# A recommendation tower on one core: what GpSimd does between rows of five gathers

## The reference, cut to what matters

```python
e = jnp.stack([tbl_0[ids[:, 0]], tbl_1[ids[:, 1]], ..., tbl_31[ids[:, 31]]], axis=1)   # 2048 x 32 x 16
row, col = _pair_indices(32)                                # the 496 pairs i < j
z = jnp.sum(e[:, row, :] * e[:, col, :], axis=2)
h = jnp.concatenate([z, dense_ctx], axis=1)                 # 2048 x 512
h = jnp.maximum(h @ W_top1 + b_top1, 0.0)                   # 512
h = jnp.maximum(h @ W_top2 + b_top2, 0.0)                   # 256
y = h @ W_top3                                              # 2048 x 1
```

## Time and profile before

| What | us |
|---|---|
| median of 3 runs | 390.6 |
| lowest, highest | 388.05, 390.77 |
| the profiled execution, whole time | 392.31 |
| its span, first to last instruction | 390.5 |
| TensorE matmuls busy, x2748 | 301.6 |
| VectorE busy | 248.0 |
| GpSimd busy | 227.9 |
| ScalarE busy | 145.0 |
| mean granted TensorE clock | 0.921 |

### The profile page before, as it was taken

The page is one execution under the profiler, slowest core; times in us unless marked ns, Lnnn a source line. Parts: engine busy times, 40 slices in busy tenths (PEclk is TensorE's granted clock), DMA queues, the critical chain, the costliest instruction groups (busy, mean ns, idle before and its releaser), DMA issues.

```text
span 390.5 us, 7439 instructions
## 1 busy us (share of the span) xinstructions
PE 301.6 (77%) x2748; PEld 278.9 (71%) x2748; DVE 248.0 (63%) x326; ACT 145.0 (37%) x311; POOL 227.9 (58%) x250
## 2 busy tenths in 40 slices
PE   1658697999777967977796797879679786978377
PEld 1348696888776857977785797768579776877366
DVE  6798769565956567394647739464673946556541
ACT  3982443434442424344242434424243441113012
POOL 6446655566656656665665666566566656657700
PEclk9988899899998999889899988989998898999759
DMA  6770020202020200102030110202012000000000
GB/s 140 207 236 5 8 64 6 65 6 64 8 63 5 64 6 15 53 6 63 5 64 6 24 44 6 63 6 64 6 17 51 6 6 5 7 8 6 7 3 1
DMA packets 19036, 14.51 MB, mean 37 GB/s; under 512 B 9727, under 2 KB 16461, under 8 KB 19022
## 3 DMA queue, kind: packets, MB, share of 16 engines
q1 hardware_dynamic: 10284, 11.69, 9.9%
q0 software_dynamic: 7680, 1.98, 6.5%
q10 hardware_dynamic: 1058, 0.66, 0.6%
HBM read 14.24 MB, written 0.08 MB: 37 GB/s over the span
## 4 chain that ended last, share of the span: by engine, by line
POOL 24%; PE 24%; issue 20%; DMA 11%; DVE 7%; another core or an unknown queue 6%; ACT 6%; SPq 1%; POOLq 0%; DVEq 0%; ACTq 0%
POOL emb L367 24%; DMA emb<-tbl,idx 10%; PE bank L663 7%; PE bank L683 6%; PE bank L645 5%; DVE emb L470 2%; PE bank L642 2%; ACT distance L844 2%; PE bank L780 1%; DVE prod L480 1%; DVE prod L489 1%; PE bank L692 1%; PE bank L699 1%; DVE mask L438 1%
## 5 line engine op out<-in xcount | busy, mean ns | idle before, releaser
L367 POOL DMA_INDIRECT emb<-tbl,idx x240 | 226.7, 945 | 141.8 <-DMA emb<-tbl,idx 80.1
L489 DVE TENSOR_TENSOR prod<-emb,bank 128x1904 f32<-128x1904 f32 (+5 forms) x51 | 94.5, 1854 | 99.3 <-DMA emb<-tbl,idx 97.3
L663 PE MATMUL bank<-ident,prod 128*128 128x128 f32 x768 | 101.9, 286 | 11.6 <-issue 4.5
L663 PEld LDWEIGHTS bank<-ident,prod 128*128 128x128 f32 x768 | 94.1, 197 | 14.3 <-issue 5.7
L683 PE MATMUL bank<-zT,w_sb 128*128 128x128 f32 x480 | 73.4, 303 | 17.7 <-ACT zT L882 16.5
L645 PE MATMUL bank<-parts,onehot 125*128 125x160 bf16 (+1 forms) x816 | 84.8, 239 | 1.8 <-issue 1.7
L683 PEld LDWEIGHTS bank<-zT,w_sb 128*128 128x128 f32 x480 | 65.9, 213 | 21.5 <-issue 19.8
L645 PEld LDWEIGHTS bank<-parts,onehot 125*128 125x128 bf16 x816 | 68.0, 104 | 1.2 <-issue 0.7
L642 PE MATMUL bank<-far_ten,named_ten 100*128 100x160 bf16 x160 | 40.9, 256 | 36.1 <-issue 26.6
L470 DVE TENSOR_REDUCE emb<-bank 128x480 f32 (+5 forms) x96 | 52.6, 583 | 10.3 <-remote 4.3
L875 ACT COPY bank<-emb 128x112 f32 (+3 forms) x32 | 7.8, 243 | 107.7 <-issue 68.4
(11 more groups left out here) (71 smaller groups left out, 137.4 us busy)
## 6 DMA issues: line engine op xcount, KB each, us to landing
gids<-small_ids_f SPq DMA_DIRECT2D x16, 544.0 KB
emb<-tbl,idx POOLq DMA_INDIRECT x240
w_sb<-w SPq DMA_DIRECT2D x1, 1024.0 KB
w_sb<-w SPq DMA_DIRECT2D x1, 512.0 KB
tab<-tbl SPq DMA_DIRECT2D x7, 56.0 KB
tab<-tbl SPq DMA_DIRECT2D x5, 70.0 KB
tab<-tbl ACTq DMA_DIRECT2D x5, 70.0 KB
z_last<-dense SPq DMA_DIRECT2D x16, 8.0 KB
```

What stands on the lines that cost most here:

```text
L367: nc.gpsimd.indirect_dma_start(emb[:, t, at:at + D], None, tables[f], bass.IndirectOffsetOnAxis(ap=idx[:, t, f:f + 1], axis=0)).then_inc(d ...
L489: return nc.vector.tensor_tensor(prod[:, at * D:(at + n * a) * D].rearrange("p (j i d) -> p j i d", j=n, d=D), strided(emb_at(t, PLACES[g] ...
L663: mm = nc.tensor.matmul(bank[:, Z_BANK + place, c * P:(c + 1) * P], v[:, d, :], ident[:], start=(d == 0), stop=(d == D - 1), is_transpose= ...
```

## The change

The wait for the landing of each fifth gather is taken out. In its place GpSimd makes six writes (memsets) of 128 x 16 float32 zeros into a new buffer `pace` that nobody reads, alternating between its two halves. Each write raises the semaphore `paced` when it is finished, and GpSimd waits for that before its next instruction. The condition on the tile changes too: the pause now stands after places 4, 9 and 14 of every tile except after place 14 of the last tile, so the last tile gets two pauses that it did not have. The number of pauses is 45 in tiles 0 to 14 as before, and 2 more; the number of writes is 47 x 6 = 282.

```diff
 RUN = 5
+WRITES = 6
...
+        pace = sb("pace", [P, 2, SUB])
...
+        paced = sem("paced")
...
                         place = GROUP_AT[g] + i - S
-                        if t < LAST_TILE and place % RUN == RUN - 1:
-                            pool.wait_ge(done, 16 * (t // 2 * n + i + 1))
+                        if place % RUN == RUN - 1 and (t, place) != (LAST_TILE, len(LARGE) - 1):
+                            for k in range(WRITES):
+                                nc.gpsimd.memset(pace[:, k % 2, :], 0.0).then_inc(paced, 1)
+                                pool.wait_ge(paced, WRITES * (len(LARGE) // RUN * t + place // RUN) + k + 1)
```

## The result

The changed kernel took **477.1 us** (median of 4, 470.5 to 481.2), against 390.3 us of the kernel before (4 runs, 388.05 to 390.77): 1.22 times as long by the medians. Two of the four runs of the changed kernel are over 1.5% slower than its fastest; without them the ratio is 1.212, with a 95% interval of 1.200 to 1.223. The forecast was 374.6 us and faster. It was wrong by 102.5 us and in its sign. The experiments will show that this is one of two answers of the same kernel: on another chip it takes 366 us. First what the trace of one of the four runs (474.3 us, span 472.5) shows.

The account below looks back on a forecast made before the run. From about tile 4 GpSimd's gathers were taken to set the pace, 22.8 us a tile. 45 pauses cut from 1.82 to 1.44 us save 17.1, less 1.1 in the last tile: 390.6 - 16.0 = 374.6 us, range 360 to 394.

Parts of the forecast that it names:

- The pause: GpSimd between two rows of five gathers: six chained writes were to take 1.44 us instead of 1.82 on average.
- The write: One GpSimd write of 16 elements in the pause: 0.12 us, between 0.10 and 0.13.
- a step: In the pause, waiting for the write before plus one write: 0.18 us (0.14 to 0.29), five times 0.90.
- the gap ahead of the gather: End of the pause, before the next row's first gather: 0.26 us, bounds 0.20 to 0.30.
- the gap behind the fifth gather: Start of the pause, between a row's last gather and the first write: 0.16 us, bounds 0.04 to 0.30.
- The sum: Whole kernel: 17.1 us saved by tile 15's first gather (at 335.0), 1.1 lost in the last tile, net 16.0 us.
- The stand of 8.72 us goes or moves: Rival, chance 0.08: ScalarE's unexplained idle stretch after the last tile's long VectorE product is lost, giving 367.0 us.
- VectorE's waits for gathers: Sign of being right: VectorE's waits for gathered rows get smaller by some 1 us a tile, not gone.
- What could absorb that gain on the way?: Step on the other engines: at 19.96 us a tile they follow, so gains up to some 30 us get through.
- Tiles of over 22 us with GpSimd ahead: Sign of being wrong: tiles running that long with GpSimd ahead would mean another engine is the bound.
- gathers whose data is still under way do not slow the ones issued behind them: Read from the last tile's 15 gathers without a pause, 17.48 us for 14 steps, 1.249 us each.
- The port lock between VectorE and GpSimd: Rival, chance 0.03: writes wait for long VectorE products, 0.5 us a pause, 23 us in all, giving 397.6 us.

Follow-up runs that it names:

- e5: The changed kernel itself (six writes a pause) run again on chip 11, with nothing altered: 365.9 us.
- e3: The kernel before without any pause, gathers issued straight on, on chip 4: 315.0 us, ratio 0.803 to the kernel before.
- e10: The kernel before without any pause, run on chip 9: 504.5 us, ratio 1.207 to the kernel before.
- e18: The kernel before with rows of seven gathers rather than five, landing wait after each seventh, no writes, on chip 3: 454.5 us, ratio 1.163.

## Why the prediction was wrong

**The pause.** Forecast 1.44 us, measured 1.24. The write took 0.112 us (forecast 0.12), a step 0.169 (0.18), the gap ahead of the gather 0.27 (0.26). The term that was off is the gap behind the fifth gather: taken as 0.16, there is none, the first write starts as the gather ends. Every third pause is 1.58 us instead, as the gather behind it waits for `made` too (a gap of 0.61 us rather than 0.27, present even where nothing is late). The 0.169 - 0.112 = 0.057 us between two writes lie within the 50 to 100 ns that the Trainium skill gives for reading a semaphore (*Advanced Engine Details and Errata*, Network/Comms). The forecast had also drawn on the Trainium skill's rule on when a writing instruction is complete (*GPSIMD Engine Reference*, Instruction dispatch), and concluded that a gap of 0.04 us behind the gather would be too small. That conclusion was wrong, as there is no gap; the rule itself is not put to the test by it, as the first write ends 0.11 us after the gather's row.

**The sum, where TensorE is free.** On chip 11 tile 15's first gather came at 332.85 (forecast 335.0) and its seventh at 341.31, which is 18.3 us earlier than 359.61 (forecast 16.0). The span was 363.5 us, and 390.5 - 18.3 - 8.7 = 363.5: the stand of 8.72 us was gone as well, as e5's timeline from VectorE's long product on shows:

```profile
343.78 2.14 DVE L495 TENSOR_TENSOR prod<-emb,bank 128x1904 f32<-128x1904 f32 x1 [5.05 <-DMA emb<-tbl,idx]
345.95 0.26 ACT L881 COPY bank<-emb 128x112 f32<-128x112 f32 x1 [5.93 <-DVE prod L495]
346.14 0.23 ACT L883 COPY emb<-emb 128x48 f32<-128x48 f32 x1
346.27 0.62 ACT L894 ACTIVATE h1T<-bank,b_sb 128x128 f32<-128x128 f32 x2
```

ScalarE's L894 starts right behind its copy, at 346.27, where before it came 8.7 us late at 373.37. So the rival "The stand of 8.72 us goes or moves", with a chance of 0.08, came true on this chip, and together with the shorter pause it makes the 365.9 us there. The work of adding up was sound, and so was the step that the other engines could do a tile in 20 us, on a free chip: e3 needs 18.7. One sign was missed even there: VectorE's waits for gathers were to shrink by 1 us a tile, and went from 97.3 to 94.7 us in all.

**The step that failed** is "What could absorb that gain on the way?" It took 19.96 us a tile from three early tiles as what TensorE, ScalarE and VectorE can do, as though that did not depend on what GpSimd does at the same time. On the chip of the measurement it does. With rows of gathers 1.24 us apart, tiles took 26 to 29 us from the fourth on, and GpSimd waited for VectorE and VectorE for TensorE. Tiles of over 22 us with GpSimd ahead were a sign of being wrong that the prediction had named. Tile 15's first gather came at 408.27 rather than 332.85, 75.4 us later, and the rest took 64.2 us rather than 30.6. Together that is the whole 109 us between the two traces of the changed kernel (472.5 and 363.5).

**The rivals.** The right one was not among them. It was nearest in "The stand of 8.72 us goes or moves". I saw a stretch in which ScalarE stood, wrote that the profile names no cause, and counted its loss as the only way in which it could matter. The rows of the profile did have the cause's mark: it was the only place of the kernel with 15 gathers in a series, and TensorE's matmuls there stood 0.7 or 1.4 us apart. The sentence "gathers whose data is still under way do not slow the ones issued behind them" was right about GpSimd and never asked about TensorE, in the same 17 us. The port lock between VectorE and GpSimd did not show: the 282 writes took 111 to 138 ns in the changed kernel and 112 to 138 in e5.

**The range** was made from the price of the pause alone. Every case in it moved with GpSimd's pace one to one, so 360 to 394 held no case in which a shorter pause costs time elsewhere.

## What to carry to other kernels

A pause that looks useless may be what keeps another engine at speed. Before shortening it, look for the one place in the trace where it is already absent, and read every engine's rows there, not only those of the engine that pauses. An unexplained stand in that place is a case with a price, and the price is paid in every tile if the change makes every tile like it. And a kernel can have two answers on two chips: here the changed kernel takes 365.3 to 366.4 us on one chip and 465.8 to 487.7 us on others, so repeating on one chip would not have shown the other answer.

## What the runs showed of the hardware

- In some sets of runs, each on one chip (that of the first measurement and chips 3, 9 and 15, but not 4, 11 and 13), TensorE is held back while GpSimd issues indirect DMAs of 128 rows of 64 bytes at one in 1.25 us. It falls from about 11 matmuls a us to 4 (17 in 4.40 us, changed kernel) or less (15 in 10.6 us, e10), in steps of 0.7 us or twice that.
- Such a stretch begins mostly 5 to 9 us after the first gather of a series (4.4 to 12.2 us in the traces of the changed kernel and of e10; the expectation of e18 has 6 to 11). In e10 it ends 1.9 to 3.4 us after the start of the last of 12 gathers, in 11 of 13 series. In the changed kernel, with its pauses of 1.24 us, it often ends before the last gather.
- The granted clock is still 1.00 when it begins and 0.50 later, after TensorE's activity has fallen, so the clock does not start it. The half clock comes on top: its mean is 0.823 in the changed kernel's trace and 0.934 in e5's.
- Removing all pauses took the kernel from 420.5 to 504.5 us on chip 9, and on chip 15, with most products zero, from 390.0 to 500.1. On chips 4 and 13 it gained 78 and 79 us (393.1 to 315.0, 393.6 to 314.6).
- GpSimd's chained writes of 128 x 16 cost 0.169 us each, and the first of them starts with no gap behind a gather.
- The kernel without pauses is the fastest that computes everything, on a free chip only. Nine writes match the kernel before on chip 3, which holds back. No version was run on both sorts of chip and found to beat the kernel before on both.
